# Attention and FFN on one core: VectorE sums key tiles 0 and 1, row maxima run one tile ahead and are transposed before they are split

## The reference

```
xn = layernorm(x)                                  # x: 4 batches x 1024 rows x 128
q, k, v = rope(xn @ Wq), rope(xn @ Wk), xn @ Wv     # 16 heads; k and v columns repeated twice
p = softmax(q @ k * scale)                          # rows of 1024 keys
attn = (p @ v) @ Wo
ffn = (silu(xn @ wg) * (xn @ wu)) @ wd              # int weights times 1/127, hidden 384
                                                    # (the FFN's x is the layernormed one)
return x + attn + ffn
```

## Time and profile before

| | |
|---|---|
| median of 3 runs | 1159.64 us |
| profiled execution | 1166.15 us |
| its span (first to last instruction) | 1164.4 us |
| TensorE busy / VectorE / GpSimd / ScalarE | 96% / 77% / 73% / 63% |
| mean granted TensorE clock | 0.984 |

### The profile page before, as it was taken

How to read it: one execution, slowest core, us unless ns; L and a number is a source line. 1 busy time by engine, 2 the same in 40 slices (tenths; PEclk the granted TensorE clock), 3 DMA queues, 4 the chain that set the end, 5 groups by cost and what they waited for, 6 DMA issues and landing times.

```text
span 1164.4 us, 17086 instructions
## 1 busy us (share of the span) xinstructions
PE 1120.0 (96%) x6288; PEld 663.2 (57%) x6288; DVE 901.1 (77%) x1023; ACT 729.8 (63%) x1327; POOL 852.9 (73%) x268
## 2 busy tenths in 40 slices
PE   5899899999999999999999999999999999999997
PEld 4787455655565555556565555555555555554443
DVE  7686877787887877788787877778787877776655
ACT  3234666666676666666676666666676666665564
POOL 3222868788788778888788778887778878887660
PEclk9899999999999999999999999999999999998889
DMA  6662908062340718062341718072341618050000
GB/s 230 159 258 77 256 2 224 1 205 58 85 141 19 207 37 224 2 205 57 96 129 26 201 37 224 1 210 53 96 130 30 196 37 224 1 130 1 5 1 19
DMA packets 56338, 124.98 MB, mean 107 GB/s; under 512 B 8000, under 2 KB 19520, under 8 KB 54080
## 3 DMA queue, kind: packets, MB, share of 16 engines
q1 hardware_dynamic: 56256, 123.90, 36.8%
HBM read 53.08 MB, written 10.49 MB: 55 GB/s over the span
## 4 chain that ended last, share of the span: by engine, by line
PE 79%; DVE 14%; SPq 2%; ACT 2%; issue 1%; DMA 1%; POOL 0%; DVEq 0%; ACTq 0%; POOLq 0%
PE bank_o L406 20%; PE bank_s L554 18%; PE scores L391 17%; DVE row_max L946 12%; PE scores L373 7%; PE bank_m L381 3%; PE bank_m L442 2%; PE bank_m L416 2%; PE bank_m L419 2%; SPq L239 2%; PE scores L492 2%; PE bank_s L509 1%; ACT prob L867 1%; PE bank_o L509 1%; DVE stats L961 1%
## 5 line engine op out<-in xcount | busy, mean ns | idle before, releaser
L946 DVE TENSOR_REDUCE row_max<-scores 128x1 f32<-128x1024 f32 x512 | 597.1, 1214 | 206.8 <-PE scores L391 206.5
L867 ACT ACTIVATE prob<-bank_s 128x512 f32<-128x512 f32 x992 | 576.7, 600 | 252.9 <-PE bank_s L554 229.5
L1181 POOL TENSOR_TENSOR prob_sum<-prob_sum,prob 128x2048 f32<-128x2048 f32 x93 | 425.7, 4577 | 13.5 <-ACT prob L867 0.5
L554 PE MATMUL bank_s<-qk_pack 98*128 98x512 f32 x992 | 415.8, 434 | 7.1 <-ACT prob L867 3.1
L391 PE MATMUL scores<-qk_pack 96*128 96x512 f32 x1024 | 337.5, 411 | 8.9 <-DVE row_max L946 0.3
L554 PEld LDWEIGHTS bank_s<-qk_pack 98*128 98x128 f32 x992 | 186.9, 189 | 184.9 <-issue 84.7
L406 PE MATMUL bank_o<-prob,v 128*32 128x512 f32 x2048 | 253.0, 612 | 0.0
L391 PEld LDWEIGHTS scores<-qk_pack 96*128 96x128 f32 x1024 | 179.5, 190 | 74.5 <-DVE row_max L946 53.0
L1181 POOL TENSOR_TENSOR prob_sum<-prob_sum,prob_pair 128x2048 f32<-128x2048 f32 x31 | 142.7, 4602 | 101.7 <-DVE prob_pair L1039 101.7
L1125 POOL TENSOR_TENSOR qk_stage<-rope,qk_stage 128x512 fp32r<-128x512 f32 x64 | 81.8, 1279 | 92.3 <-ACT qk_stage L753 92.3
L1173 POOL TENSOR_TENSOR prob_sum<-prob 128x2048 f32<-128x2048 f32 x31 | 142.2, 4586 | 0.0
(11 more groups left out here) (105 smaller groups left out, 742.4 us busy)
## 6 DMA issues: line engine op xcount, KB each, us to landing
qk_pack<-qk_stage SPq DMA_DIRECT2D x384, 128.0 KB, 5.0
table<-tables SPq DMA_DIRECT2D x16, 2048.0 KB, 9.6
w_stage<-w_scratch SPq DMA_DIRECT2D x14, 640.0 KB, 4.5
v<-v_stage SPq DMA_DIRECT2D x32, 256.0 KB, 8.1
xT_scratch<-xT_hl SPq DMA_DIRECT2D x4, 1024.0 KB, 9.5
x_stage<-xT_scratch SPq DMA_DIRECT2D x4, 1024.0 KB, 7.0
w_scratch<-w_split SPq DMA_DIRECT2D x1, 2560.0 KB, 15.1
x_all<-x SPq DMA_DIRECT2D x4, 512.0 KB, 11.7
```

Of the source, the lines that this page charges most:

```text
L554: mm(bank_s[:, h % 2, :], qk_pack[j][0:SCORE_K, 1, kt // QT, h, (kt % QT) * 128:(kt % QT + 1) * 128], qk_pack[j][0:SCORE_K, 0, t, h, :], s ...
L867: A(prob[:, kt % RING, h, :], bank_s[:, h % 2, :], ACT.Exp).then_inc(prob_ready, 1)
L946: V.tensor_reduce(row_max[:, m:m + 1], scores[:, at:at + 2, :].rearrange("p c k -> p (c k)"), axis=AX.X, op=ALU.max).then_inc(max_read, 1)
L1181: TT(prob_sum[:, t], prob_sum[:, t], part, ALU.add).then_inc(sum_done, 1)
```

## The change

- `pair_sum` on VectorE adds key tiles 0 and 1, writes `prob_sum` directly, and stands after the eighth reduction of the slot (`PAIR_AFTER = 7`). GpSimd waits for it and adds tiles 2, 3, 4, 5 and 6, again five additions. `prob_pair` is gone.
- Tile 0 of the maxima of unit v+1 is issued by TensorE at the end of slot u, so all maxima stand one tile earlier than before. In the first slot, which has no tile issued ahead, one more is issued in kt 5.
- `row_max` is transposed as it is (16 rows), directly after s(6,1); ScalarE writes the high part from PSUM (`high_max`), VectorE the low part (`low_max`, between the two chunks of `rotate`), and each row is moved by a transfer of its own.
- `transpose_inv` stands behind s(5,1), `invert` after reduction 10, `round_hi` of both chunks and `read_y` change places on ScalarE.

```diff
-INVERT_AFTER = 9
+INVERT_AFTER = 10
+PAIR_AFTER = 7
 ...
             def pack_max(v, n, t):
-                sp.wait_ge(maxT_read, v + 1)
-                sp.dma_start(qk_pack[n][SPLIT_K:SCORE_K, 0, t]..., max_rows[:]).then_inc(max_packed, 16)
+                for r, ready in enumerate((max_hi, max_lo)):
+                    sp.wait_ge(ready, v + 1)
+                    sp.dma_start(qk_pack[n][SPLIT_K + r:SPLIT_K + r + 1, 0, t]..., max_rows[r][:]).then_inc(max_packed, 16)
 ...
             def transpose_max(v):
-                pe.wait_ge(max_lo, v + 1)
-                nc.tensor.transpose(bank_m[0:2 * TILES, 0:128], max_hl[:]..., ident[:]).then_inc(maxT_ready, 1)
+                pe.wait_ge(max_read, TILES * v + TILES)
+                at_least(pe, max_lo, v)
+                nc.tensor.transpose(bank_m[0:TILES, 0:128], row_max[:], ident[:]).then_inc(maxT_ready, 1)
 ...                                               # end of kt 7 on TensorE
-                            pe.wait_ge(maxT_read, v + 1)
+                            pe.wait_ge(max_lo, v + 1)
                             project_v(w, t, blocks=range(QT // 2))
 ...
                         score(kt, 3)
+                        if t == 0 and v + 1 < UNITS:
+                            pe.wait_ge(packed, 16 * PACKS * (s + 1))
+                        maxima(v + 1, 1 - j, t)
 ...                                               # ScalarE
-            def read_maxT(v):
+            def high_max(v):
                 act.wait_ge(maxT_ready, v + 1)
-                nc.scalar.copy(max_rows[:], bank_m[0:2 * TILES, 0:128]).then_inc(maxT_read, 1)
+                nc.scalar.copy(max_rows[0][:].bitcast(F32R), bank_m[0:TILES, 0:128]).then_inc(max_hi, 1)
 ...
-                        if (kt, h) == (0, 2) and not first and staged:
-                            stage_v(u + 3, 1 - t, s + 1 + t)
+                        if (kt, h) == (0, 2) and staged:
+                            if not first:
+                                stage_v(u + 3, 1 - t, s + 1 + t)
+                            round_hi(0, u + 3, 1 - t, s + 1 + t)
 ...
                         elif (kt, h) == (1, 1) and staged:
-                            round_hi(0, u + 3, 1 - t, s + 1 + t)
-                        elif (kt, h) == (1, 3) and not is_second(u):
-                            read_y(u - 2)
+                            round_hi(1, u + 3, 1 - t, s + 1 + t)
                         elif (kt, h) == (2, 1):
-                            if staged:
-                                round_hi(1, u + 3, 1 - t, s + 1 + t)
+                            if not is_second(u):
+                                read_y(u - 2)
                             if not first:
                                 read_den(u - 1)
 ...                                               # VectorE
-            def split_max(v):
-                V.tensor_copy(max_hl[:, 0, :].bitcast(F32R), row_max[:]).then_inc(max_hi, 1)
-                V.tensor_tensor(max_hl[:, 1, :], row_max[:], max_hl[:, 0, :], ALU.subtract).then_inc(max_lo, 1)
+            def low_max(v):
+                dve.wait_ge(max_hi, v + 1)
+                V.tensor_tensor(max_rows[1][:], bank_m[0:TILES, 0:128], max_rows[0][:], ALU.subtract).then_inc(max_lo, 1)
 ...
-            def pair_sum(u):
-                dve.wait_ge(prob_ready, NE * (KT * u + 6))
-                V.tensor_tensor(prob_pair[:], prob[:, 4 % RING], prob[:, 5 % RING], ALU.add).then_inc(pair_done, 1)
+            def pair_sum(u, t):
+                dve.wait_ge(prob_ready, NE * (KT * u + 2))
+                V.tensor_tensor(prob_sum[:, t], prob[:, 0], prob[:, 1], ALU.add).then_inc(pair_done, 1)
 ...                                               # GpSimd
             def add_probs(u, t):
-                ...                               # tiles (0, 1), 2, 3, pair, 6
+                pool.wait_ge(pair_done, u + 1)
+                for n, kt in enumerate(range(2, KT - 1)):
+                    pool.wait_ge(prob_ready, NE * (KT * u + kt + 1))
+                    TT(prob_sum[:, t], prob_sum[:, t], prob[:, kt % RING], ALU.add).then_inc(sum_done, 1)
```

More of the change, by code:

```diff
@@ L105, in build @@
         row_max = keep("row_max", [128, TILES])
-        max_hl = keep("max_hl", [128, 2, TILES])
-        max_rows = keep("max_rows", [2 * TILES, 128])
+        max_rows = [keep(f"max_rows{n}", [TILES, 128]) for n in range(2)]
         o_raw = keep("o_raw", [128, HALF])
@@ L541, in _ @@
             pe.wait_ge(filled, 2)
+            tiles = [iter(range(TILES)) for _ in range(UNITS)]
             def slot(i, j, t, last_pair):
@@ L547, in slot @@
                 v_n, v_t = (j, 1) if t == 0 else (1 - j, 0)
-                do_max = not (last_pair and j == 1 and t == 1)
-                tiles = iter(range(TILES))
                 def score(kt, h):
@@ L565, in pv_pair, with maxima @@
                         pv(u - 1, KT - 1, j if t == 1 else 1 - j)
-                def maxima():
-                    if do_max:
-                        m = next(tiles)
+                def maxima(v=v, v_n=v_n, v_t=v_t):
+                    if v < UNITS:
+                        m = next(tiles[v])
                         if m < 2:
-                            pe.wait_ge(rope_done, capped(2 * u + 7 + m, 2 * UNITS))
+                            pe.wait_ge(rope_done, capped(2 * v + 5 + m, 2 * UNITS))
                         max_tile(v, m, v_n, v_t)
@@ L632, in slot @@
                         score(kt, 3)
+                    elif kt == 5:
                         maxima()
[L634 removed]
+                        score(kt, 1)
                         if not is_first(u):
                             transpose_inv(u - 1)
[L637 to L638 removed]
                         score(kt, 2)
@@ L641, in slot @@
                         score(kt, 3)
+                        if is_first(u):
+                            maxima()
                     elif kt == 6:
@@ L882, in slot @@
                             spread_inv(u - 1)
-                        elif (kt, h) == (6, 2) and not (last_pair and j == 1 and t == 1):
-                            read_maxT(u + 1)
+                        elif (kt, h) == (6, 1):
+                            high_max(u + 1)
             def body(i, last_pair):
@@ L929, in _, with rotate @@
             V = nc.vector
-            def rotate(w, t, s):
+            def rotate(w, t, s, pairs=range(2)):
                 at_least(dve, lo_done, 2 * w)
                 dve.wait_ge(table_in, 16 * (s + 1))
-                for k in range(2):
+                for k in pairs:
                     dve.wait_ge(proj_ready, 5 * w + 2 * k + 1)
@@ L1052, in slot @@
                 u = 4 * i + 2 * j + t
-                do_max = not (last_pair and j == 1 and t == 1)
-                if do_max:
-                    for m in range(TILES):
-                        reduce_tile(u + 1, m)
-                        if m == INVERT_AFTER and not is_first(u):
-                            invert(u - 1)
-                    split_max(u + 1)
-                else:
-                    invert(u - 1)
+                for m in range(TILES):
+                    reduce_tile(u + 1, m)
+                    if m == PAIR_AFTER:
+                        pair_sum(u, t)
+                    if m == INVERT_AFTER and not is_first(u):
+                        invert(u - 1)
                 if not is_first(u):
                     normalise(u - 1)
-                pair_sum(u)
                 if not last_pair:
-                    rotate(u + 4, t, 2 * i + j + 2)
+                    rotate(u + 4, t, 2 * i + j + 2, (0,))
+                low_max(u + 1)
+                if not last_pair:
+                    rotate(u + 4, t, 2 * i + j + 2, (1,))
             def body(i, last_pair):
@@ L1120, in _, with split_lo @@
             TT = nc.gpsimd.tensor_tensor
-            def split_lo(w, t):
-                for k in range(2):
+            def split_lo(w, t, chunks=range(2)):
+                for k in chunks:
                     pool.wait_ge(hi_done, 2 * w + k + 1)
@@ L1192, in slot @@
                 u = 4 * i + 2 * j + t
-                if not (last_pair and (j, t) != (0, 0)):
+                staged = not (last_pair and (j, t) != (0, 0))
+                if staged:
                     split_lo(u + 3, 1 - t)
```

71 lines of the change are left out of this document (24 added, 47 removed).

## The result

The changed kernel takes 1181.31 us (median of 4 runs, 1180.18 to 1183.33), the kernel before on the same chip 1159.24 us (4 runs). The ratio is 1.0171, 95% interval [1.014, 1.0203]: slower, though the interval leaves open whether by less or more than 2%. The forecast was 1161 us and no change, and the time lies outside the range.

The account below looks back on a forecast made before the run. TensorE was taken as the bound, with a share where it follows VectorE. Terms +3.8 (steady slots), -0.9 (start) and -1.5 (last slots) gave +1.4 us on 1166.15, carried to the median: 1161 us, range 1148 to 1175.

Parts of the forecast that it names:

- -0.60 + 0.74 = +0.14 us: Steady slot on TensorE: kt 5 stretch shortens by 0.60, slot-start stretch grows by 0.74; +3.8 us over 27 slots.
- a bank is free 1.1 us after its last score, three times 0.09 short, 0.28 in all: In kt 5, scores s(4,3) and s(5,0) side by side wait for ScalarE, 0.28 us in all.
- The stall of tile 2: At the slot's start tile 2 waits until VectorE has read tile 0, starting 1.90 us behind it; 0.27 loss.
- Slot 0 starts 0.7 us later ... I take -0.9: First slot: later start, one more tile, idle time absorbing it; +0.5, or -1.8 if the half clock is avoided; taken -0.9.
- the cover of the denominators: Pair sum behind the eighth reduction hides beside kt 2's PV pair and the denominators: cost 0, margin 0.8 us.
- -0.5 each, -1.5: Slots 28 to 30: the tile ahead fills the wait for the maxima; -1.5 us, between 0 and -3 each if clock stays up.
- the rival on the shared port: Slower: GpSimd's operation holds the moved pair sum on VectorE, deciding from 0.8 us of delay; 1173 us, chance 0.16.
- the margin: Time between the moved pair sum's end at 549.4 and the ninth tile's reduction due at 550.2: 0.8 us.
- The cast that the prediction counts beside it: VectorE's 128x16 cast, 0.90 us, ending with GpSimd's 4.66 us addition; taken as a sign that GpSimd holds such operations.
- The faster rival: Waits for VectorE mostly go because it has 3.1 us less behind the reductions; -0.36 per slot, 1148 us, chance 0.26.
- The rival of the late low row: Slower: the low row's transfer reaches the first score late, deciding from 3.1 us between issue and use; 1180 us, chance 0.11.

Follow-up runs that it names:

- e6: The changed kernel with ScalarE taking only half the width of the seven exponentials (4,2) to (6,0): 1166.87 us, ratio 1.0046 to the kernel before.
- e5: The changed kernel with VectorE reducing only half the columns of maximum tile 0: 1163.7 us, ratio 1.0023 to the kernel before.
- e3: The changed kernel with one maximum tile fewer before a slot's first PV pair and four in kt 5 again: 1165.13 us, ratio 1.0026 to the kernel before.
- e8: The changed kernel with the pair sum of slot 0 alone one reduction earlier: 1178.39 us, ratio 1.0147 to the kernel before.
- e1: The changed kernel with the tile issued ahead undone, its other parts kept: 1165.5 us, ratio 1.0026 to the kernel before.
- e2: The kernel before with only the tile issued ahead added; pair sum, split and transfers as before: 1192.9 us, ratio 1.0258.
- e4: The changed kernel with the pair sum of key tiles 4 and 5 back at the slot's end, tile ahead kept: 1176.44 us, ratio 1.0115 to the kernel before.

## Why the prediction was wrong

**The steady slot: right in sign, wrong in size.** The step "-0.60 + 0.74 = +0.14 us" failed; it measured -0.38 + 0.85 + 0.03 (the projections) + 0.02 (the rest) = +0.52.
- *s(4,2) to the PV pair.* The term "a bank is free 1.1 us after its last score, three times 0.09 short, 0.28 in all" was mis-sized. I took the handover at each pair of scores apart. ScalarE never gets ahead: the seven exponentials run as one chain at 0.63 us each, and the wait is 0.50 (4.18 less TensorE's 3.68), one half at each of the two pairs of scores side by side. e6 takes it away. How much of the 0.63 is the exponential and how much the handover is not shown. (The terms that the prediction adds up for TensorE's own distances give 3.66, not 3.68; the slip changes nothing.)
- *s(7,3) to s(0,2).* The stall of tile 2 was found and nearly sized: 1.94 behind tile 0, forecast 1.90. The 0.11 beyond is mostly what follows it: 0.57 from tile 2 to s(0,2), where 0.47 stands only behind matmuls that queue without a gap. e5 takes the stall away, e3 moves the tile.
- The small amounts count 27 times: 0.38 us per slot missed is most of the error in the trace, 9 us of 15.5 by the distances (12.8 against 3.8; 27 x 0.52 would be 14.0, but two of before's distances are themselves longer, 33.34 and 32.98). Outside the trace, carrying the difference from the profiled execution to the median missed another 5 us.

**The start: wrong in sign.** The step "Slot 0 starts 0.7 us later ... I take -0.9" measured +3.2 up to the first `normalise`: +0.55 before slot 0, +3.85 by the lower clock from s(0,0) to s(2,2), +1.2 from there to the first score of slot 1 (the wait of 2.36, the lower clock behind it and the tile ahead, less before's wait of 2.45), and -2.4 in slot 1, whose first PV pair no longer runs at the lower clock. The forecast had the first (0.7) and had thought of the last; two terms stood at nothing. I had costed the pair sum at nothing by the cover of the denominators and applied that to all slots; slot 0 has none, and e8 shows that this costs 3.5. The fall of the clock at the beginning of slot 0 I did not have at all; e1 and e2 show with which part it goes, and its cause stays open.

**The last slots: not gained.** "-0.5 each, -1.5" measured +0.9 over three distances. In the changed kernel the tile ahead did not keep the clock up; it fell at other places. The idea behind the term is not refuted by that: in e4, with the same tile ahead, the clock stayed up there and the three distances are 92.8 us against before's 96.6. The term was a gain that comes in some kernels and not in others, and nothing here says in which.

**What held.** The pair sum costs nothing in the steady slot (e1, e4). It took 2.55 us in place of 2.28; in slot 0, with no `add_out` beside it, it took its old time:

```profile
127.29 2.28 DVE L1036 TENSOR_TENSOR prob_sum<-prob 128x2048 f32<-128x2048 f32 x1
```

In the steady slot it began at 557.53, inside `add_out` (556.65 to 557.93), as the rival on the shared port had it, and the delay of 0.27 stayed under the margin: VectorE was still idle for 0.53 us before the next reduction, so that rival fell on its own condition. The Trainium skill, "SBUF — State Buffer", "Who interferes with whom", has the later of the two operations wait; the trace agrees here in place and direction. (The cast that the prediction counts beside it has one SBUF input, of which the rule as told there does not speak; what stands is that it ended with GpSimd's addition, at 530.23 and 530.19 before, and again in e2, at 541.71 and 541.67.) `low_max` took 0.27 (taken 0.29), and no first score of a steady slot waited for the transfer of a row. GpSimd's additions ended at 528.43 + 23.51 = 551.94, 5.6 us into the slot that begins at 546.33, as forecast, in part by luck: they began 15.3 us into their slot in place of 14.9 and took 0.2 longer, and the longer slot took that up. The faster rival fell: VectorE's freed 3 us became idle time, most of it in front of the rope. The rival of the late low row had 1180 us as its price, close to the measured 1181; that is chance, for no first score of a steady slot waited for a row.

The range was too narrow because it was built from single mechanisms. All three misses went the same way, and the rivals for "slower" rested on a held pair sum and a late row, when the terms to doubt were the tile itself and the slots without a cover.

## What to carry to other kernels

Count each stretch between two covers by the slowest of its producers and consumers, not by the busiest engine's own distances: from the third tile on at the reducing engine's pace, scores side by side at the activation engine's pace. Before you cost a move at nothing, name the cover in every form of the loop body, the first and the last too, where the cover may be missing. Time freed on an engine counts only if someone waits for it at that place: here 3 us of VectorE per slot were worth 0 without the tile ahead; with it the split's part was worth 0.6 and the pair sum's still 0, and that did not pay for the tile.

## What the runs showed of the hardware

- Seven exponentials of 128x512 from PSUM in a row ran in 4.43 us (0.63 each, 0.599 shown for one); two at 552.05 us in the changed kernel took 1.10 together, 0.50 apart. Of 128x256 one took 0.38 (e6).
- A cast of 128x16 took 0.90 us before and 1.69 in e2. Both began inside a 4.66 us addition of GpSimd and ended with it, while the following subtraction of the same size took 0.17. A sum of 128x2048 took 2.28 us with GpSimd idle (slots 0 and 1) and 2.54 to 2.56 where it began inside a 1.28 us operation of GpSimd (from slot 2 on).
- A single wait of 2.36 us in slot 0 was followed by TensorE at the lower clock (maximum tile 1.05 in place of 0.73). At the end of slot 28, waits of 0.35 and 0.22 us were followed by it in one kernel and, with 0.35 and 0.21, not in another. At the beginning of slot 0 waits of 1.05 and 0.88 us were followed by it in the changed kernel, and waits of 0.91 and 0.88 not in the kernel before.
